# Two attentions of a four-layer kernel: the split of the row maxima moves from DVE to Pool, and TensorE gets unused products in a third step

## The reference

```
# L0_xattn_ref(ctx, ctx, layernorm(x)):      16 heads of width 8
energy = jnp.einsum('nqhd,nkhd->nhqk', q, k)
attn = jax.nn.softmax(energy / jnp.sqrt(jnp.float32(EMBED_SIZE)), axis=3)
out = jnp.einsum('nhql,nlhd->nqhd', attn, v).reshape(N, q_len, EMBED_SIZE)
return out @ w_out.T + b_out
# L1_xattn_ref(layernorm(x), ctx, ctx): the same with projections of q, k, v and scale 1/sqrt(8)
```

## Time and profile before

| | |
|---|---|
| median of 3 runs | 609.9 us (609.39 to 614.12) |
| the profiled execution: its own time | 611.74 us |
| the profiled execution: span | 609.9 us |
| PE busy | 524.9 us (86%) |
| DVE busy | 364.6 us (60%) |
| ACT busy | 301.6 us (49%) |
| POOL busy | 84.1 us (14%) |
| mean granted clock of TensorE | 0.947 of full |

### The profile page before, as it was taken

One profiled execution on the slowest core, in us unless ns is written; L12 is line 12 of the kernel. 1 busy time (PEld: TensorE's weight loads), 2 busy tenths in 40 slices (PEclk: granted clock), 3 DMA queues, 4 the chain that ended last, 5 costly groups with the idle time before them and its releaser, 6 DMA issues.

```text
span 609.9 us, 8855 instructions
## 1 busy us (share of the span) xinstructions
PE 524.9 (86%) x3219; PEld 287.7 (47%) x3222; DVE 364.6 (60%) x948; ACT 301.6 (49%) x495; POOL 84.1 (14%) x81
## 2 busy tenths in 40 slices
PE   6889987999968999877977649999999947887997
PEld 2234433667823344343734213455556626543665
DVE  6777816162568686279243647878785387542644
ACT  7356762433111578426355337877776024552421
POOL 4000001000000000007073099200000140000000
PEclk9888998999998699998999779999999998999999
DMA  4688000034025000000000000000000500000000
GB/s 141 192 252 375 2 24 7 1 85 124 0 80 159 23 2 3 1 0 1 0 1 0 2 0 1 0 1 2 1 1 2 206 0 2 1 2 1 0 1 18
DMA packets 11466, 26.15 MB, mean 43 GB/s; under 512 B 2112, under 2 KB 6592, under 8 KB 10784
## 3 DMA queue, kind: packets, MB, share of 16 engines
q1 hardware_dynamic: 11424, 25.59, 12.8%
HBM read 22.44 MB, written 3.15 MB: 42 GB/s over the span
## 4 chain that ended last, share of the span: by engine, by line
PE 61%; DVE 21%; issue 7%; ACT 6%; POOL 3%; DMA 1%; SPq 0%; POOLq 0%; DVEq 0%; ACTq 0%
DVE mxs L832 5%; PE ps L1625 5%; PE ps L1535 5%; PE ps L1519 5%; PE ps L1508 5%; PE ps L1634 5%; PE ps L1877 5%; PE ps L1453 4%; PE ps L1355 4%; PE ps L1387 3%; PE ps L1886 2%; ACT Kst L612 2%; DVE xn L783 2%; POOL rstd L464 2%; PE ps L1569 1%
## 5 line engine op out<-in xcount | busy, mean ns | idle before, releaser
L832 DVE TENSOR_REDUCE mxs<-ps 128x1 f32<-128x512 f32 x128 | 81.2, 680 | 22.6 <-PE ps L1355 22.6
L547 ACT ACTIVATE PR<-ps 128x1024 f32<-128x1024 f32 x80 | 76.6, 973 | 33.2 <-PE ps L1387 17.0
L463 POOL TENSOR_SCALAR ve<-mv 128x4 f32<-128x4 f32 x11 | 2.6, 235 | 401.8 <-DVE mv L771 345.0
L1355 PE MATMUL ps<-Kst,Qst 84*128 84x512 bf16 x128 | 46.9, 420 | 11.6 <-DVE mxs L832 6.3
L914 DVE TENSOR_REDUCE nm<-ps 128x1 f32<-128x512 f32 x64 | 41.0, 683 | 23.5 <-PE ps L1508 23.5
L1588 PE MATMUL ps<-ctxT,const_t 128*128 128x512 f32 x90 | 42.2, 615 | 5.7 <-DMA const_t<-in_const 5.7
L596 ACT ACTIVATE Qst<-ps,nm 128x512 f32<-128x512 f32 x64 | 45.4, 709 | 2.8 <-DVE nm L914 2.7
L588 ACT COPY PR<-ps 128x512 f32<-128x512 f32 x64 | 37.9, 595 | 17.2 <-PE ps L1519 17.2
L556 ACT COPY Qst<-ps 12x1024 bf16<-12x1024 bf16 x24 | 24.0, 1001 | 44.9 <-PE ps L1426 44.9
L1387 PE MATMUL ps<-Qst,Kst 84*128 84x256 bf16 x256 | 42.1, 291 | 0.3
L354 DVE SCALAR_TENSOR_TENSOR x<-ps,comb,x 128x128 f32<-128x128 f32 x64 | 18.0, 344 | 39.4 <-PE ps L1634 32.5
(11 more groups left out here) (330 smaller groups left out, 898.2 us busy)
## 6 DMA issues: line engine op xcount, KB each, us to landing
Kst<-k_rows SPq DMA_DIRECT2D x48, 96.0 KB
FC<-in_fc SPq DMA_DIRECT2D x2, 2048.0 KB, 12.2
Qst<-q_rows SPq DMA_DIRECT2D x48, 48.0 KB
FC<-in_w SPq DMA_DIRECT2D x1, 2048.0 KB, 7.6
k_rows<-REP SPq DMA_DIRECT2D x12, 128.0 KB, 3.0
REP<-in_w SPq DMA_DIRECT2D x1, 1536.0 KB, 7.0
q_rows<-REP SPq DMA_DIRECT2D x20, 64.0 KB, 2.0
FC<-in_w2e SPq DMA_DIRECT2D x1, 1024.0 KB, 9.6
```

The source lines that it names most:

```text
L547: act.activation(PRg[:, g % 2, u * 1024:u * 1024 + width], bank(3 + 2 * (n % 2), 2)[:, 0:width], ACT.Exp, scale=scale).then_inc(s.p_ready, 1)
L832: i = dve.tensor_reduce(m[:, u // 4, u % 4:u % 4 + 1], bank(n % 2), AX_X, ALU.max)
L1355: i = pe.matmul(bank(n % 2), Qst[0:ROWS_A, b, h, q0:q0 + P], Kst[0:ROWS_A, b, h, :], start=True, stop=True)
```

## The change

In attentions 0 and 1 the split of the maxima is taken out of DVE's queue. Pool does it, in a new function `split_max(a)`, with five linked operations (a negation by a multiplication with -1, the rest by an addition, the second part, the rest, the third part). Pool waits for the eight reductions of the group (`smax_read`) and, from the third group of all, until `mp`'s buffer has been turned (`m_turned`). DVE gets a wait at the start of steps 2 to 7 for the split of two steps before, since `mxs` has two buffers. `split_max(0)` stands in Pool's queue behind the copy into `Vaug`, `split_max(1)` behind `rstd_of(3)`. The third attention keeps the split on DVE. Apart from that, PE gets two unused products a part in step 2, into bank 7, so they now run in the first three steps.

```
+            def split_max(a):
+
+                for g in range(G):
+                    m = mxs[:, g % 2, :, :]
+                    to = mp[:, g % 2, :, :, :]
+                    r = mr[:, :].rearrange("p (t h) -> p t h", t=2)
+                    pool.wait_ge(s.smax_read, MAXB[a] + 8 * (g + 1))
+                    if groups(a, g) >= 2:
+                        pool.wait_ge(s.m_turned, groups(a, g) - 1)
+                    link(pool.tensor_scalar(to[:, :, 0, :], m, -1.0, None, ALU.mult))
+                    link(pool.tensor_tensor(r, m, to[:, :, 0, :], ALU.add))
+                    link(pool.tensor_scalar(to[:, :, 1, :], r, -1.0, None, ALU.mult))
+                    link(pool.tensor_tensor(r, r, to[:, :, 1, :], ALU.add))
+                    pool.tensor_scalar(to[:, :, 2, :], r, -1.0, None, ALU.mult).then_inc(s.m_ready, 1)
+                    pool.wait_ge(s.m_ready, groups(a, g) + 1)
+
+            split_max(0)
             rstd_of(1)
             rstd_of(2)
             rstd_of(3)
+            split_max(1)
             rstd_of(4)
...
                 for step in range(G + 4):
+                    if a < 2 and 2 <= step < G:
+                        dve.wait_ge(s.m_ready, groups(a, step) - 1)
                     for part in range(8):
...
-                    if step < G:
+                    if step < G and a == 2:
 
                         m = mxs[:, step % 2, :, :]
                         to = mp[:, step % 2, :, :, :]
...
-                        if a < 2 and step < 2:
-                            for _ in range(3):
-                                pe.matmul(bank(6), identb[:, :], Kparts[:, 0, 0:SK] if a == 0 else onesel[:, :, :],
+                        if a < 2 and step < 3:
+                            for _ in range(3 if step < 2 else 2):
+                                pe.matmul(bank(6 if step < 2 else 7), identb[:, :], Kparts[:, 0, 0:SK] if a == 0 else onesel[:, :, :],
                                           start=True, stop=True)
```

## The result

The changed kernel takes 605.8 us (median of 20 runs, 601.3 to 611.1), the kernel before 611.97 us (20 runs beside them, 609.06 to 614.23; its first three had given 609.9). The ratio is 0.990 (0.988 to 0.992), 6.2 us faster. Executions more than 1.5% above the fastest of their kernel are left out of the ratios, though not of the medians: one of these 20, the profiled one and five more of e2's twelve, the profiled one of e9, and four of the kernel before beside e9 and e10. The profiled execution took 605.59 us, span 603.8 us, against 611.74 and 609.9. Forecast were 599.4 and a fall of 10.5 us: the direction held, the size did not. Of the 6.4 us between 599.4 and 605.8, 2.1 lie in the base (609.9 in three runs, 611.97 in twenty), the other 4.3 in the change's worth.

A forecast was written before the change was run, and what follows sets the result against it. It took TensorE as the bound from step 3 on, at half clock in step 3; -4.45 us (first attention) and -6.05 (second) made -10.5, median 609.9 to 599.4 us, range 596.5 to 606.

The forecast's parts named there:

- The clock is what matters in step 3: Step 3 of both attentions: products in step 2 hold the full clock, 11.3 us becomes 6.3, gain 5.0 us each.
- Steps 4 to 7 gain next to nothing: Full steps, PE the bound: without DVE's split each gains only 0.06 us, 0.2 us per attention.
- 0.56 us at the border of steps 0 and 1: Between steps 0 and 1: without DVE's split the first reduction starts at 25.49 and not 26.05, gaining 0.56 us.
- Step 2 becomes 6.1 us: Step 2 with eight unused products: four parts and the turn come to 6.1 us, 0.15 us longer than before.
- Pool's split takes 1.5 us: Pool's five linked split operations take 1.5 us, covered in full steps before PE's turn of the maxima.
- Rival 3: PE's turn of the maxima in every step: Pool's split outlasts its cover, total 621 us; chance 0.04.
- attention 1's term, -6.05: Whole second attention: sum of -0.56, +0.15, -5.0, -0.45 and -0.2, so 6.05 us shorter.
- attention 0's "+1.05 us" for the late first split: First attention, step 1: Pool's first split waits behind the copy of the values, so the step ends 1.05 us later.
- rival 2: First attention: PE's wait for Pool drops the clock during step 2; total -6 to -7.5, 602 to 604 us; chance 0.16.
- bank cycling: Before the clock's fall in step 3: PE alternating between two score banks with short idling (0.42 us) makes the clock swing.
- The time behind the attentions: Everything behind: same work, shifted earlier; clock falls there may come out longer or shorter, 2.5 us either way.

The follow-up runs named there:

- e2: The changed kernel without the unused products in step 2, so only the split moves to Pool; 608.54 us, ratio 0.989 to the kernel before.
- e9: The changed kernel measured once more, unaltered; 605.64 us, ratio 0.992 to the kernel before.
- e10: The kernel of e5 with two unused products a part in steps 0 and 1 in place of three; 600.94 us, ratio 0.989 to the kernel before.
- e7: The kernel before with Pool splitting only groups 0 to 2 of attention 1, no products in step 2; ratio 0.989 to the kernel before.
- e8: The kernel before with Pool splitting only groups 3 to 7 of attention 1, no products in step 2; ratio 1.000 to the kernel before.
- e3: The changed kernel with the copy into Vaug behind the first split in Pool's queue; 601.79 us, ratio 0.984 to the kernel before.
- e4: The changed kernel with 14 more unused products on PE ahead of attention 0's turn that waits for Pool; 607.81 us, ratio 0.993 to the kernel before.
- e5: The kernel of e3 without any unused products in step 2; 598.27 us, ratio 0.981 to the kernel before.
- e1: The kernel before with only the eight unused products in step 2 of both attentions, DVE keeping the split; 604.86 us, ratio 0.988 to the kernel before.

## Why the prediction was right and wrong, point by point

- **The clock is what matters in step 3** held: 11.3 us became 6.71 in both attentions. The term was 5.0 us an attention, and is 4.6: a full step has 6.7 us also without the turn of the outputs. The low stretch that it prices, 10.2 us, is not a fixed one: it took 3.4 us in attention 0 of e7 and 13.7 in e8.
- **Steps 4 to 7 gain next to nothing** held, even more so: a full step takes 6.72 us (47.48 to 54.20) against 6.70. The 0.06 us was wrong, since at a step's start a reduction begins 0.49 us after its product without any split too. DVE's row in the changed kernel, whose product is that of 54.20:

```profile
54.69 1.89 DVE L850 TENSOR_REDUCE mxs<-ps 128x1 f32<-128x512 f32 x3 [0.73 <-PE ps L1375]
```

- **0.56 us at the border of steps 0 and 1** held: attention 1's step 2 starts 11.90 us after its first product (182.56 to 194.46) and not 12.44.
- **Step 2 becomes 6.1 us** held (6.08).
- **Pool's split takes 1.5 us** held (1.47); its cover was never used up in attention 1, where Pool is done 2.1 to 2.8 us ahead of PE's turn. Rival 3 falls.
- So attention 1's term, -6.05, came out at -5.3.
- **The term that failed is attention 0's "+1.05 us" for the late first split, with "the clock up".** I had seen the place and the copy that makes it late, and priced only the delay. Three things were off. PE came to the turn at 27.84 us and not at 28.99, since the low clock of the attention's first products (the row below, of the kernel before), which I had taken over from the profile, was absent in this execution; that is luck of the execution, and e9 has the low start again. The copy came 0.4 us later. And the standing PE lost its clock. The wait was 3.2 us, and a low stretch of 6.8 us followed (a clock of 0.51 and 0.50 in the windows from 30.0 to 36.8). e3 prices it all: 70.44 - 65.01 = 5.4 us. At the turn the change is 3.3 us behind e3, counted from the attention's start (31.05 - 18.47 against 28.15 - 18.84), and at the end another 2.2; e4, where PE is busy in the same delay and keeps its clock, says that the second part is the clock. This is rival 2, whose chance I put at 0.16, with a total of -6 to -7.5 that the 6.2 us fit; it was there in both profiled executions of the change, and in e2. A fall so early is no proof by itself: in e8, whose attention 0 is that of the kernel before, the clock also fell in step 2 (at 33.8 us). What carries the point is that e3, e4 and e5, where PE does not stand still, kept 1.00 there.

```profile
19.25:22.66 3.41, 3.41 (x10) 1.08 (x9) 2.38 (x4) 0.95 (x1) 0.00 (x0) 0.50 0.61 186
```

- **What the forecast had not in it at all:** that the relief of DVE holds the clock by itself. The sum booked 0.2 us an attention for it, and the 5.0 to the products; in attention 1 either alone holds the clock, and the relief alone gives more (6.3 us against 3.75). I read DVE's split as harmless because in full steps it hides behind PE. In step 2 and at the border to step 3 it does not, and the 0.42 us pause that I quoted as a sign of bank cycling was a wait for DVE behind its split. e2, e5 and e7 show that taking the split away holds the clock; that it does so through these short pauses is argued, from PE's busy time and from e1, where products fill most of them with the same effect. No single pause decides: e1 keeps one of 0.43 us in step 3 (ahead of 39.12) and its clock holds. The Trainium skill, page "TensorE: Matmul & The Clock Gate", section "Why this matters for your kernels", names only long idle gaps as what drops the clock. That is contradicted here: the clock fell behind pauses of 0.6 us and less, and holds in attention 1 of e7, where none in those steps is longer than 0.21. The same page of the Trainium skill, section "A second HAM failure mode: psum-queue depth-cycling", has the clock swing through brief idling between groups of products. With the idling the traces agree; the cycling itself does no harm, since PE goes through the same two banks in e5 with the clock at 1.00.
- **The time behind the attentions** was allowed 2.5 us either way. The experts took 90.03 to 93.86 us and the part behind 355.18 to 360.47 in the twelve profiled executions with the same instructions there. In a 72 us stretch of it the clock was 0.98 in the kernel before (488 to 560) and 0.91 in e3 (478 to 550, nearly the same work):

```profile
488.00:560.00 72.00, 53.52 (x517) 33.85 (x517) 42.19 (x129) 31.99 (x48) 7.01 (x10) 0.98 0.01 1
```

That these parts go with the clock is seen; why a given execution gets the long or the short form is open.

By the profiled executions: forecast -4.45 and -6.05, found -1.1 and -5.3, and +0.3 for the rest, together -6.1.

## What to carry to other kernels

When work moves to another engine, look at what stands ahead of the first piece in that engine's queue: the later pieces had 2.1 to 2.8 us of cover left, the first one was waited for 3.2 us, and moving one copy behind it was worth 5.4 us of that attention. An engine that seems to be off the critical path in full steps can still thin out TensorE's work in the ramp before them, and where the clock falls there, that step or the next is paid at double price. Before filling such gaps with unused products, take away what makes them: here the relief alone was faster than relief and products together.

## What the runs showed of the hardware

- A low clock can go on while PE is busy: 10.2 us in step 3 of the kernel before, with PE at work all the time.
- Pool does five linked operations of eight elements per partition in 1.47 us, an addition in 0.20, a multiplication by a constant in 0.23; the power of four elements took 1.04.
- In e9 a wait of 1.65 us on PE had a low clock behind it, from 32.8 us, 1.9 us after its end; the same place filled with products (e4) kept the full one.
